# P V products of two key blocks together in the slots that hold no experts pieces, of one block in the others

## The reference, cut to what matters

```python
# x: (4, 1024, 512) f32, 16 heads of 32; experts: 8, rank 64
xq, xk, xv = ((x @ w.T).reshape(4, 1024, 16, 32) for w in (wq, wk, wv))
scores = jnp.einsum('bqhd,bkhd->bhqk', xq, xk)
probs = softmax(scores)
out = jnp.einsum('bhqk,bkhd->bqhd', probs, xv).reshape(4, 1024, 512)
x = layernorm(x + out @ wo.T)
logits = x_flat @ Wr.T + br                  # router, best expert per token
h = jnp.einsum('nd,erd->ner', x_flat, A)     # (tokens, 8, 64)
y = jnp.einsum('ner,eor->neo', h, B) / 64
x = layernorm(x + y[best expert] * softmax(logits)[best expert])
```

## Time and profile before

| | |
|---|---|
| time, median of 3 runs | 1638.07 us (1634.61 to 1640.32) |
| the profiled execution's own time | 1635.75 us |
| its span, first to last instruction | 1634.0 us |
| PE busy | 1571.7 us, 96% |
| POOL, DVE, ACT busy | 1176.5, 941.6, 768.9 us |
| mean granted clock of TensorE | 0.996 |

### The profile page before, as it was taken

The page is one execution under the profiler, slowest core; times in us unless marked ns, Lnnn a source line. Parts: engine busy times, 40 slices in busy tenths (PEclk is TensorE's granted clock), DMA queues, the critical chain, the costliest instruction groups (busy, mean ns, idle before and its releaser), DMA issues.

```text
span 1634.0 us, 19390 instructions
## 1 busy us (share of the span) xinstructions
PE 1571.7 (96%) x6432; PEld 754.4 (46%) x6432; DVE 941.6 (58%) x1689; ACT 768.9 (47%) x1409; POOL 1176.5 (72%) x657
## 2 busy tenths in 40 slices
PE   7999999999999999999999999999999999999898
PEld 3444444444444444444444444444444444444354
DVE  2656665654565567655456556755545777764343
ACT  1155555554455444445445544444544555555332
POOL 0078989987877677667788766786777888989711
PEclk9999999999999999999999999999999999999999
DMA  6534543344122322134332133313423222210001
GB/s 200 147 109 115 160 118 91 85 111 123 29 77 71 79 85 74 44 105 123 97 98 45 35 85 91 84 40 91 149 47 91 46 47 59 60 40 21 7 1 52
DMA packets 82083, 132.09 MB, mean 81 GB/s; under 512 B 18608, under 2 KB 36032, under 8 KB 81984
## 3 DMA queue, kind: packets, MB, share of 16 engines
q1 hardware_dynamic: 79776, 126.12, 28.1%
q0 software_dynamic: 1152, 4.22, 0.8%
q10 hardware_dynamic: 1056, 0.52, 0.1%
HBM read 87.84 MB, written 42.20 MB: 80 GB/s over the span
## 4 chain that ended last, share of the span: by engine, by line
PE 85%; DVE 6%; issue 3%; POOL 2%; DMA 2%; ACT 1%; SPq 1%; ACTq 0%; POOLq 0%
PE sc L585 15%; PE pv L597 14%; PE w L484 14%; PE mx L575 14%; PE w L495 7%; PE w L547 5%; PE w L506 5%; PE w L534 5%; DVE mxc L763 2%; DVE eq L846 1%; PE w L528 1%; POOL Psum L417 1%; PE w L541 1%; PE mx L547 1%; ACT P L652 1%
## 5 line engine op out<-in xcount | busy, mean ns | idle before, releaser
L763 DVE TENSOR_REDUCE mxc<-mx 128x1 f32<-128x512 f32 x1024 | 684.3, 686 | 548.3 <-PE mx L575 545.0
L417 POOL TENSOR_TENSOR Psum<-Psum,P 128x1024 f32<-128x1024 f32 x384 | 901.8, 2367 | 117.7 <-ACT P L652 113.2
L652 ACT ACTIVATE P<-sc 128x512 f32<-128x512 f32 x1024 | 593.3, 596 | 609.5 <-PE sc L585 606.3
L585 PE MATMUL sc<-stack 98*128 98x512 f32 x1024 | 675.4, 661 | 9.9 <-DMA stack<-mrow 5.4
L575 PE MATMUL mx<-stack 96*128 96x512 f32 x1024 | 414.8, 408 | 8.1 <-DVE mxc L763 8.0
L585 PEld LDWEIGHTS sc<-stack 98*128 98x128 f32 x1024 | 193.5, 189 | 289.1 <-issue 136.2
L484 PE MATMUL w<-xT_s,wqk_s 128*128 128x512 f32 x512 | 267.3, 613 | 13.6 <-DMA wqk_s<-wkT 11.1
L575 PEld LDWEIGHTS mx<-stack 96*128 96x128 f32 x1024 | 195.6, 191 | 173.9 <-issue 137.8
L597 PE MATMUL pv<-P,V 128*32 128x512 f32 x2048 | 272.8, 605 | 0.0
L413 POOL TENSOR_TENSOR Psum<-P 128x1024 f32<-128x1024 f32 x64 | 151.2, 2369 | 153.5 <-ACT P L652 146.5
L484 PEld LDWEIGHTS w<-xT_s,wqk_s 128*128 128x128 f32 x512 | 93.1, 193 | 96.0 <-issue 78.8
(11 more groups left out here) (114 smaller groups left out, 820.9 us busy)
## 6 DMA issues: line engine op xcount, KB each, us to landing
stack<-qk_parts SPq DMA_DIRECT2D x192, 256.0 KB, 5.4
qk_parts<-split SPq DMA_DIRECT2D x64, 512.0 KB, 2.8
xT_s<-xT SPq DMA_DIRECT2D x8, 1024.0 KB, 9.4
den_s<-den_parts SPq DMA_DIRECT2D x124, 64.0 KB, 2.0
r<-x SPq DMA_DIRECT2D x3, 2048.0 KB, 8.5
out<-r SPq DMA_DIRECT2D x12, 512.0 KB, 3.1
wqk_s<-wqT SPq DMA_DIRECT2D x15, 256.0 KB, 4.2
wqk_s<-wkT SPq DMA_DIRECT2D x15, 256.0 KB, 4.5
```

What stands on the lines that cost most here:

```text
L417: pool.tensor_tensor(Psum[:, s % 2, i, :], Psum[:, s % 2, i, :], P[:, unit % NP, :], ALU.add).then_inc(add_done, 1)
L585: pe.matmul(sc[c][:, :], stack(s, i)[0:KS, 0, 128 * kb:128 * kb + 128], stack(s, i)[0:KS, 1, 512 * c:512 * c + 512], start=True, stop=True ...
L652: act.activation(P[:, unit % NP, 512 * c:512 * c + 512], sc[c][:, :], ACT.Exp).then_inc(exp_done, 1)
L763: dve.tensor_reduce(mxc[:, q % 2, m:m + 1], mx[TURN[g] % NMX][:, :], AX.X, ALU.max).then_inc(mx_done, 1)
```

## The change

The order of P V blocks on PE, and nothing else. A new function `blocks(s, k)` names the blocks of slot s that are issued in the second half of unit k, where k goes on through the next slot as 16 + k. In slots whose number within the batch is 2 to 6, from batch 1 on (those with experts' pieces), blocks stay one at a time, at odd k from 3. In all others they come in twos at k = 5, 9, 13 and 17: blocks 0 and 1 in half 11, 2 and 3 in half 19, 4 and 5 in half 27, 6 and 7 in half 3 of the next slot. That is 17 slots with 4 pairs, 68 pairs. Number and shape of the matmuls, banks, buffers and semaphores stay.

```diff
+    def blocks(s, k):
+
+        if s >= PAIRS and 2 <= s % PAIRS < PAIRS - 1:
+            return ((k - 3) // 2,) if k % 2 and k >= 3 else ()
+        return ((k - 5) // 2, (k - 3) // 2) if k % 4 == 1 and k >= 5 else ()
...
-                if c == 1 and k == 1 and s:
-                    out_block(s - 1, KB - 1)
-                if c == 1 and k % 2 == 1 and k >= 3:
-                    out_block(s, (k - 3) // 2)
+                if c == 1 and s:
+                    for kb in blocks(s - 1, UNITS + k):
+                        if kb < KB:
+                            out_block(s - 1, kb)
+                if c == 1:
+                    for kb in blocks(s, k):
+                        out_block(s, kb)
...
-            out_block(LAST, KB - 1)
+            for kb in blocks(LAST, UNITS + 1):
+                out_block(LAST, kb)
```

## The result

The changed kernel takes 1618.72 us (median of 4 runs, 1616.95 to 1620.56) against 1636.74 us of the kernel before on the same occasions: ratio 0.9889, 95% interval 0.9872 to 0.9905, so 1.1% or 18 us faster. 1620 were forecast, with a range of 1615 to 1629.

The account below looks back on a forecast made before the run. PE's stream was taken as the bound, with POOL's floor close in batch 0 and POOL last in slot 31. Stretch gains of 18.3 us less 1.0 gave 17.3, from 1635.75 us 1618.5, from the median 1620.8: 1620 us, range 1615 to 1629.

Parts of the forecast that it names:

- What bounds the kernel: In the slots with 24 chunks PE alone sets the pace: whatever leaves its stream leaves the time.
- sign of being wrong: Wrong if slots 2 to 6's scores wait markedly longer for exponentials, or clock behind slot 6's/7's start falls below 1.00.
- A block alone: A single P V block on PE costs 1.19 us: two passes of 0.45 us, 0.29 us at its edges.
- the lower bound I named: A pair's second block costs 0.85 us if its passes step by 0.43 us; 0.90 was taken.
- The first rival: The second block waits for its weights: 0.20 us saved per pair, 1626 us; chance 0.12.
- The stretches: Gains by slots: 0-1 3.2, 2-4 3.8, 5-6 1.7, 7-10 2.6, 15-18 with 23-26 7.0, together 18.3 us.
- Start of slot 2: Up to the first chunk, half 11: 0.6 us more idle inside PE's 1.62 us wait for x, gain 0.
- The clock: Idle before slots 6 and 7 grows to 1.4 us; a drop costs 1.5 us each; part of a 0.12 rival.
- The opposite rival: Halves without a chunk fall to DVE's pace, lacking a free `mx` bank: net 11 us slower, 1649; chance 0.05.
- lumpiness: Halves without P V cover between pairs: 0.1 us at about ten places in slots 3 to 6, 1.0 us off.

## Why the prediction was right

- **What bounds the kernel.** Right. The gain came from PE's stream alone, and one matmul between the blocks took it away. The scores of slots 2 to 6 don't wait for exponentials longer than before, and behind the starts of slots 6 and 7 the clock held: neither sign of being wrong is there.
- **A block alone, 1.19 us, of which 0.29 edges.** The 1.19 are right. The edges are 0.34: I took a pass at 0.45 us, the distance within a lone block, and it is 0.43 between blocks and inside the second one. The 0.02 us belong to the entry. The 0.85 us of the second block was the lower bound I named.
- **The rule of the Trainium skill** ("TensorE: Matmul & The Clock Gate", Part 3, "The mechanism") that a weight load overlaps only matmuls on other row groups doesn't hold here, taken by itself. All loads use all 128 rows and the second block follows without a gap. The first rival, made from it, is refuted by the 2.52 us.
- **The stretches.** The slots with 24 chunks gave more than forecast, 12.3 instead of 9.6 us. With 0.34 us my counts make 11.4: 37 pairs, 12.6, less the block of 1.19 that moves from slot 6 into slot 7. The other 0.9 us aren't accounted for. Slots 0 and 1 gave 3.8, with 0.34 us 3.6. Slot 31 gave nothing, as forecast: PE's idle time before the sums grew from 3.68 to 4.58 us.
- **Start of slot 2, the step that failed.** I put it at 0: the first chunk would stay at its distance from the slot's start, come 3.2 us earlier and wait 1.0 us for x. It came 1.8 us earlier and didn't wait. I took x's transfer to be issued at the slot's start. In the kernel, SP first issues the loads of later stacks, for which it waits until the last score of slot 1 is done, and x's transfer behind them. Half 31 has lost its block, so slot 2 starts 1.2 us sooner behind that score. SP's timelines in slot 2, before and after, and PE's in the kernel with slot 31 put back:

```profile
159.81 2.94 SPq L311 DMA_DIRECT2D stack<-qk_parts  x6
...
165.84 1.48 SPq L274 DMA_DIRECT2D xT_s<-xT  x2
...
157.67 2.94 SPq L318 DMA_DIRECT2D stack<-qk_parts  x6
...
162.79 2.17 SPq L281 DMA_DIRECT2D xT_s<-xT  x2
...
172.89 1.10 PE L491 MATMUL w<-xT_s,wqk_s 128*128 128x512 f32 x2 [1.01 <-issue]
```

  The stacks' loads start 1.62 us ahead of the slot's start before (161.43), and 0.42 us ahead of it after (158.09). x lands 13.5 us behind the start before and 14.6 after, and the chunk can't come earlier: that is 1.0 us. In the third trace, where the clock holds, PE stands 1.01 us waiting for it. The late stack also met a PE that came sooner, with no block in half 7: it idled 0.99 us, in the changed kernel's trace the clock fell behind that, and the chunk came at 15.2 us instead of 14.6. With the bank in slot 3, told of below, slots 2 to 4 gave 1.9 instead of 3.8 us; at 0.34 us a pair it would have been 4.3.
- **The closing part, left out.** 3.1 us came back behind the last score. I had counted slot 31 as zero and not thought of what comes behind it. Some 0.6 us are PE's longer way to the sums (10.6 instead of 10.0 us), which the pairs cause; the rest is low clock, whose length differs between traces of the same order in slot 31 (104.9 and 106.6 us for the whole part), so its cause stays open.
- **The clock.** I looked for its fall at the starts of slots 6 and 7, where it held; it fell in slot 2, behind less idle time than the 1.62 us that had left it alone before. That the start of slot 6 held was no sure thing: behind 1.22 us idle it held in this trace and fell in that of the kernel with blocks beside den.
- **The opposite rival**, halves waiting for DVE's reduces, is seen at one place of weight, in slot 3, and cost 0.9 us there (in slot 6 PE idles 0.22 us at the same point). It isn't DVE's pace that does it. DVE stood 1.91 us at the reciprocal of the sums, whose transfer was under way, and the reduces queued behind it; with no block left in half 15, PE came to the max matmul of half 17 before a bank was free. Two timelines, of DVE and of PE:

```profile
216.72 0.25 DVE L796 RECIPROCAL spread_s<-spread_s 128x16 f32<-128x16 f32 x1 [1.91 <-DMA spread_s<-den_s]
216.89 2.42 DVE L774 TENSOR_REDUCE mxc<-mx 128x1 f32<-128x512 f32 x4
...
217.57 0.50 PE L582 MATMUL mx<-stack 96*128 96x512 f32 x1 [0.66 <-DVE mxc L774]
```


So the mechanism was right, and that the number came so close was luck. At 0.34 us a pair my counts give 21.3 us; the traces give 16.8. Slots 2 to 4 lost 2.3 us of it, the closing part 3.1, the later start of the loop 0.5, and 1.4 us came in elsewhere. That I had the saving 3.0 us too small over 59 pairs, and took 1.0 us off for lumpiness, cancelled these losses. The forecast of 17.3 us is better than its terms.

## What to carry to other kernels

Price what stands at the edges of a matmul of another array shape, from start to start, and bring those of one shape together; a single full matmul between them pays everything again. Before an instruction is moved, look at what it covers: den had hidden the emptying of a bank, and its move by half a step cost 28 us, while moving its neighbours to it gained 18.6. When work leaves a place, look at the next thing PE meets there, a landing, a bank, or a small DVE instruction, and not only at the wait that is on the list already. And look up which instruction a transfer waits for: x's stood behind loads that wait for the last score of slot 1, and a block that left the place behind that score brought the next slot 1.2 us nearer to it.

## What the runs showed of the hardware

- Groups of four matmuls of 128 x 32 follow each other at the full pace of the passes (0.85 to 0.87 us a block, across a change of `pv` to `w` bank as well); the change to or from full-width matmuls costs 0.34 us in all.
- Two small DVE instructions of the experts, the comparison and the gate (128 x 8), took 0.2 to 0.3 us, or up to 2.4 and even 5.0 us when they met POOL's instructions. In the changed kernel's trace 28 of these 64 last over 1 us, and every one ends 0.02 to 0.03 us behind the end of a POOL instruction, 25 adds and 3 products. The reduces and reciprocals of the same chain, on 8 columns or one, also in SBUF, never took over 0.17 us. The Trainium skill ("SBUF — State Buffer", "Summary: rules for kernel authors") has the rule that, where DVE is in its two-port mode, or has two SBUF inputs while GpSimd's instruction reads SBUF, the second one to issue fully blocks until the first is done. The comparison has two SBUF inputs (`lsb` and `rank`), and the trace agrees: 10 of its 12 long ones start behind the start of the add that they end with, and the one of 5.0 us starts 0.3 us before the end of an add and lasts through the two that follow. The gate has one full input and two columns of scalars, and no run shows in which mode it went. None of this was tried by taking the adds away.
- Idle times of 0.99 us were followed by the low clock in one trace, and of 1.62 us not in another. The same place can go either way: behind the stack's wait in slot 2 the clock fell after 0.99 us in the changed kernel and held after 0.91 us in the kernel with slot 31 put back. What else decides it is open.
